# Issuing both stores and then all four loads of a two-batch round, with A and B fetched four batches ahead

## The chip, the core and the metric

The kernel runs on one core of one Trainium2 chip. The metric is device time in microseconds (us) of one execution. The core has a matmul engine (TensorE, PE in the profile), VectorE (DVE), ScalarE (ACT), GpSimd (POOL), and SyncE (SP), which here issues every transfer. All transfers of the loop go through one queue that 16 DMA engines serve. TensorE's granted clock is 1.00 of full speed, that is 2.4 GHz, in every stretch of the loop.

## What is computed

`x` is 64 batches of 128 channels by 2048 time steps, float32. Each batch gets one of 16 conditioning matrices added as a residual, and then one of 64 low-rank adapters (rank 16), again as a residual:

```python
W = weights[condition]                       # (64, 128, 128)
x = x + jnp.einsum('bct,bcd->bdt', x, W)
B_req = B[adapter_ids]                       # (64, 16, 2048)
A_req = A[adapter_ids]                       # (64, 2048, 16)
Bx = jnp.einsum('bni,bri->bnr', x, B_req)    # rank-16 image of each row
x = x + jnp.einsum('bnr,bor->bno', Bx, A_req)
```

For each batch 1024 KB of x come in, 256 KB of A and B (laid side by side by the host) come in, and 1024 KB go out.

## The kernel before

The work is cut into rounds of two batches (ROUND = 2), two rounds to a loop turn (BODY = 4), so 32 rounds in all. They are called r0 to r31 here; round r works on batches b = 2r and b + 1. Four buffers each exist of the input (`x_in`), the output (`x_out`), the A-and-B tile (`ab_in`) and the turned A (`at`); batch b uses number b modulo 4.

TensorE in round r does: `mix_units` for both batches (L376: x times the identity plus W, which gives the first residual F, in four units of 512 columns), `sum_z` for both (L392: F times B, which gives the rank-16 rows z), then `add_low_rank` for the two batches of the round before (L410: A times z). ScalarE copies F out of its banks (L264) and half of z. VectorE in round r, in its program order: `take_z` (L311) for both batches, `add_units` (L318: low-rank part plus F into `x_out`, four units for each batch) for the two batches of the round before, `turn_a` (L327: the transpose of A into `at`) for the two batches of round r. GpSimd picks the matrices and sums the pieces of z.

SyncE follows one order written out by hand in `turn` (L171 to L186) and each of its steps may block all that stand behind it:

- `store(k, b)` waits for the four `add_units` of batch b, then writes batch b out (L159).
- `next_x(k, b)` waits until batch b - 4 has been mixed (`f_made`), then loads x of batch b into the same buffer (L128).
- `next_ab(k, b)` reads the adapter's number, waits for `sum_z` (`z_done`) and `turn_a` (`a_turned`) of batch b - 4, then loads A and B of batch b (L131).

In round r, with b = 2r, the order is: store b - 4, load x of b + 4, store b - 3, load A and B of b + 2 and of b + 3, load x of b + 5. So x is asked for two rounds ahead of its use, A and B one round ahead.

The waits at the other end: `mix_units` waits for `x_loaded`, `sum_z` and `turn_a` for `ab_loaded`, `add_low_rank` for `a_turned`, and `add_units` for `stored`, the landing of the store from the same `x_out` buffer four batches before. The last two batches (from L438 on TensorE, L347 on VectorE) are interleaved by hand.

Of the kernel before, what the change touches and what calls it, by code (L numbers as in the profile page):

```python
# [10 lines left out]
BATCHES, CHANNELS, TIME = 64, 128, 2048  # L11
# [15 lines left out]
ROUND = 2  # L27
BODY = 2 * ROUND
# [11 lines left out]
TURNS = BATCHES // BODY  # L40

def live(count):

    return not (isinstance(count, int) and count <= 0)

def begun(b):

    return not (isinstance(b, int) and b < 0)  # L50
# [7 lines left out]
def cond_lora_residual(nc, x, both_ids, weights, lora, out):  # L58
    with ExitStack() as ctx:
# [57 lines left out]
        def rows_of_z(z_bank, c):  # L117
            return bank[z_bank][TILE * c:TILE * c + RANK, 0:P]
# [3 lines left out]
        @block.sync  # L122
        def _(sp):
            def adapter_of(b):
                return sp.value_load(ids[0:1, 1, bass.ds(b, 1)], min_val=0, max_val=lora.shape[0] - 1)  # L125

            def load_x(k, b):
                sp.dma_start(x_in[k][:], x[b]).then_inc(x_loaded[k], 16)  # L128

            def load_ab(k, adapter):  # L130
                sp.dma_start(ab_in[k][:], lora[adapter]).then_inc(ab_loaded[k], 16)  # L131

            def load_first(i):
                cols = slice(UNIT * i, UNIT * (i + 1) if i < 2 else TIME)
                sp.dma_start(x_in[0][:, cols], x[0, :, cols]).then_inc(first_loaded[i], 16)

            def load_w_first(k):
                cond = sp.value_load(ids[0:1, 0, k:k + 1], min_val=0, max_val=CONDITIONS - 1)  # L138
                sp.dma_start(w_first[k][:], weights[:, cond, :]).then_inc(w_first_in[k], 16)

            sp.dma_start(ids[:].rearrange("p n b -> p (n b)"), both_ids).then_inc(ids_in, 16)
            load_first(0)
            sp.wait_ge(ids_in, 16)
            load_w_first(0)
            load_first(1)
            load_first(2)
            load_w_first(1)
            load_x(1, 1)
            for k in range(ROUND):
                load_ab(k, adapter_of(k))  # L150
            sp.dma_start(w_all[:], weights).then_inc(w_in, 16)
            for k in range(ROUND, BODY):
                load_x(k, k)
            for k in range(ROUND, BODY):
                load_ab(k, adapter_of(k))

            def store(k, b):
                sp.wait_ge(added, UNITS * (b + 1))
                sp.dma_start(out[b], x_out[k][:]).then_inc(stored[k], 16)  # L159

            def next_x(k, b):
                sp.wait_ge(f_made, UNITS * (b - BODY + 1))
                load_x(k, b)

            def next_ab(k, b):
                adapter = adapter_of(b)
                sp.wait_ge(z_done, b - BODY + 1)
                sp.wait_ge(a_turned, b - BODY + 1)
                load_ab(k, adapter)

            def turn(q, last):  # L171
                for kind in range(KINDS):
                    k, other = ROUND * kind, ROUND * (1 - kind)
                    b = BODY * q + k
                    if begun(b - BODY):
                        store(k, b - BODY)
                    if not last:
                        next_x(k, b + BODY)
                    if begun(b - BODY):
                        store(k + 1, b + 1 - BODY)  # L180
                    if begun(b - ROUND) and not (last and kind > 0):
                        next_ab(other, b + ROUND)
                        next_ab(other + 1, b + ROUND + 1)
                    if not last:
                        next_x(k + 1, b + 1 + BODY)

            turn(0, False)
            with sp.Fori(1, TURNS - 1) as q:
                turn(q, False)
            turn(TURNS - 1, True)  # L190

            def store_last(u):
                cols = slice(UNIT * u, UNIT * (u + 1))
                sp.dma_start(out[BATCHES - 1, :, cols], x_out[BODY - 1][:, cols]).then_inc(stored[BODY - 1], 16)

            for k in range(BODY - 1):
                store(k, BATCHES - BODY + k)
            for u in range(1, UNITS):
                sp.wait_ge(evacuated, u)
                store_last(u)  # L200
            sp.wait_ge(added, UNITS * (BATCHES - 1) + 1)
            store_last(0)
            for k in range(BODY):
                sp.wait_ge(stored[k], 16 * (TURNS if k < BODY - 1 else TURNS - 1 + UNITS))
# [99 lines left out]
        @block.vector  # L304
        def _(dve):
            def take_z(i, b, z_bank):
                dve.wait_ge(z_done, b + 1)
                if live(b - 1):
                    dve.wait_ge(z_paired, 2 * (b - 1))
                for c in (1, 3):  # L310
                    nc.vector.tensor_copy(z_part[i][c][:], rows_of_z(z_bank, c)).then_inc(z_taken_dve, 1)  # L311

            def add_units(k, b, turns, banks, units=range(UNITS)):
                if live(turns):
                    dve.wait_ge(stored[k], 16 * turns)
                dve.wait_ge(low_done, b + 1)
                for u in units:
                    nc.vector.tensor_tensor(x_out[k][:, UNIT * u:UNIT * (u + 1)], bank[banks[u]][:], ft[k][u][:],  # L318
                                            ALU.add).then_inc(added, 1)

            def turn_a(k, b, turns):
                dve.wait_ge(ab_loaded[k], 16 * turns)
                if live(b - BODY + 1):
                    dve.wait_ge(low_done, b - BODY + 1)
                flat = ab_in[k][:, 0:JS * RANK + RANK]
                blocks = bass.AP(flat.tensor, flat.offset, [flat.ap[0], [RANK, JS], [1, BLOCK]])
                nc.vector.transpose(at[k][:], blocks).then_inc(a_turned, 1)  # L327

            def normal_round(kind, q):
                b = BODY * q + ROUND * kind  # L330
                for i in range(ROUND):
                    take_z(i, b + i, Z_BANKS[i])
                if begun(b - ROUND):
                    for i in range(ROUND):
                        add_units(ROUND * (1 - kind) + i, b - ROUND + i, q - (kind == 0), LOW_BANKS[kind][i])
                for i in range(ROUND):
                    turn_a(ROUND * kind + i, b + i, q + 1)

            def turn(q):
                for kind in range(KINDS):  # L340
                    normal_round(kind, q)

            turn(0)
            with dve.Fori(1, TURNS - 1) as q:
                turn(q)
            normal_round(0, TURNS - 1)
            take_z(0, BATCHES - 2, Z_BANKS[0])  # L347
            add_units(0, BATCHES - 4, TURNS - 1, LAST_LOW)
            turn_a(BODY - 2, BATCHES - 2, TURNS)
            turn_a(BODY - 1, BATCHES - 1, TURNS)  # L350
            add_units(1, BATCHES - 3, TURNS - 1, LAST_LOW, (0, 1))
            take_z(1, BATCHES - 1, Z_BANKS[0])
            add_units(1, BATCHES - 3, TURNS - 1, LAST_LOW, (2, 3))
            add_units(BODY - 2, BATCHES - 2, TURNS - 1, LAST_LOW)
            add_units(BODY - 1, BATCHES - 1, TURNS - 1, LAST_OWN, (0,))
# [129 lines left out]
```

## Time and profile before

| what | us |
|---|---|
| median of 3 runs | 410.05 |
| lowest, highest | 408.6, 418.84 |
| the profiled execution, its own time | 412.59 |
| its span, first to last instruction | 410.8 |

| engine | busy in the span |
|---|---|
| TensorE matmul | 373.9 us, 91% |
| VectorE | 229.9 us, 56% |
| ScalarE | 238.1 us, 58% |
| GpSimd | 113.6 us, 28% |
| DMA, one queue on 16 engines | 95.0% of their time, 152.19 MB |

The profile is a record of one execution, so sums made from it are made against its own time of 412.59 us. Matmul busy time is a weak measure by itself, as matmuls overlap and their ends are modelled; the distances between the starts of rounds are the better measure. DMA shares are the time that packets took, as a share of 16 engines, and can come out slightly over 1. The time "to landing" of a transfer runs from its issue by SyncE to the last of its completions, so it holds the queueing too.

### The profile page before, as it was taken

What the parts mean: (1) busy time and instruction counts of PE and PEld (TensorE: products, weight loads), DVE (VectorE), ACT (ScalarE), POOL (GpSimd) and SP (SyncE); (2) the same over time, 40 slices, a digit from 0 to 9 for tenths busy, and PEclk for the clock granted to TensorE, in tenths of its full rate; (3) what the DMA queues carried; (4) which work ended last, traced back from release to release, by engine and by line L of the source; (5) the groups of instructions that cost most, each with busy time, mean ns of one, the idle gap of its engine ahead of it and who ended that gap; (6) DMA issues with size and microseconds to landing.
All of it is one profiled execution on the core that took longest, in us unless ns stands there. A gap on an engine that the chain in (4) does not pass through costs nothing.

```text
span 410.8 us, 16881 instructions
## 1 busy us (share of the span) xinstructions
PE 373.9 (91%) x6164; PEld 354.5 (86%) x6164; DVE 229.9 (56%) x445; ACT 238.1 (58%) x580; POOL 113.6 (28%) x263
## 2 busy tenths in 40 slices
PE   8889999999999999999989989898997998989871
PEld 8779999999999999999989979798886897878771
DVE  0116776555566677655556765466753566535762
ACT  2366666656666666665656655566554665546541
POOL 1123333332222333332213333123331133312320
PEclk9899999999999999999999999999999999999995
DMA  6998999999999999999999999999999899999546
GB/s 186 410 372 293 395 409 415 413 412 409 400 408 416 420 410 407 399 421 422 368 422 381 391 416 340 420 335 412 381 350 381 302 410 356 343 392 372 227 167 253
DMA packets 28815, 152.37 MB, mean 371 GB/s; under 512 B 3201, under 2 KB 3458, under 8 KB 12546
## 3 DMA queue, kind: packets, MB, share of 16 engines
q1 hardware_dynamic: 28802, 152.19, 95.0%
q8 instruction: 9, 0.15, 0.1%
q14 instruction: 4, 0.03, 0.0%
HBM read 85.07 MB, written 67.11 MB: 370 GB/s over the span
## 4 chain that ended last, share of the span: by engine, by line
PE 58%; DMA 30%; SPq 4%; issue 3%; DVE 2%; ACT 1%; POOL 1%; ACTq 0%; POOLq 0%; DVEq 0%
PE bank L376 35%; DMA ab_in<-in_lora 28%; PE bank L410 12%; PE bank L392 11%; DMA x_in<-in_x 2%; DVE x_out L318 1%; SPq L125 1%; SPq L159 1%; SPq L128 1%; POOL z_pair L226 0%; DMA ids<-in_ids 0%; DVE z_part L311 0%; SPq L138 0%; ACT x_out L302 0%; SPq L131 0%
## 5 line engine op out<-in xcount | busy, mean ns | idle before, releaser
L376 PE MATMUL bank<-m_sel,x_in 128*128 128x128 f32 x2048 | 240.8, 278 | 3.9 <-DMA x_in<-in_x 2.2
L376 PEld LDWEIGHTS bank<-m_sel,x_in 128*128 128x128 f32 x2048 | 234.1, 193 | 8.7 <-DMA x_in<-in_x 2.6
L264 ACT COPY ft<-bank 128x512 f32<-128x512 f32 x256 | 145.6, 588 | 60.1 <-PE bank L376 58.7
L318 DVE TENSOR_TENSOR x_out<-bank,ft 128x512 f32<-128x512 f32 x253 | 154.3, 680 | 18.5 <-PE bank L410 18.5
L311 DVE COPY z_part<-bank 16x128 f32<-16x128 f32 x128 | 36.8, 287 | 155.1 <-PE bank L392 152.4
L226 POOL TENSOR_TENSOR z_pair<-z_part 16x128 f32<-16x128 f32 x128 | 55.0, 446 | 232.3 <-DVE z_part L311 212.4
L276 ACT COPY z_all<-z_all 16x128 f32<-16x128 f32 x192 | 56.9, 296 | 49.8 <-POOL z_all L231 46.7
L392 PE MATMUL bank<-ft,ab_in 128*16 128x128 f32 x2048 | 64.0, 273 | 20.0 <-DMA ab_in<-in_lora 19.7
L392 PEld LDWEIGHTS bank<-ft,ab_in 128*16 128x16 f32 x2048 | 52.5, 96 | 27.5 <-issue 22.2
L410 PE MATMUL bank<-z_all,at 16*128 16x128 f32 x2048 | 70.0, 284 | 2.5 <-DVE x_out L318 2.5
L410 PEld LDWEIGHTS bank<-z_all,at 16*128 16x128 f32 x2048 | 63.7, 189 | 9.5 <-issue 9.3
L271 ACT COPY z_part<-bank 16x128 f32<-16x128 f32 x128 | 32.9, 257 | 52.3 <-PE bank L392 50.0
L327 DVE STREAM_TRANSPOSE at<-ab_in 128x512 f32<-128x512 f32 x64 | 41.3, 682 | 0.0
L217 POOL TENSOR_TENSOR m_sel<-w_all,ident 128x128 f32<-128x128 f32 x62 | 28.4, 457 | 37.9 <-PE bank L376 19.4
L231 POOL TENSOR_TENSOR z_all<-z_pair 16x128 f32<-16x128 f32 x64 | 28.5, 446 | 7.4 <-POOL z_pair L226 4.5
L418 PE MATMUL bank<-ident 128*128 128x128 f32 x20 | 4.6, 429 | 1.6 <-POOL ident L210 1.6
L418 PEld LDWEIGHTS bank<-ident 128*128 128x128 f32 x20 | 4.3, 331 | 1.6 <-POOL ident L210 1.6
L302 ACT COPY x_out<-bank 128x512 f32<-128x512 f32 x3 | 1.6, 594 | 2.5 <-PE bank L410 2.5
L238 POOL TENSOR_TENSOR m_sel<-w_first,ident 128x128 f32<-128x128 f32 x2 | 0.9, 458 | 6.7 <-DMA w_first<-in_weights 6.7
L264 ACT ACT_TABLE_LOAD x1 | 1.3, 1283 | 0.8 <-PEq L470 0.8
L210 POOL TENSOR_SCALAR_AFFINE_SELECT ident<-ident 128x128 f32<-128x128 f32 x1 | 0.3, 294 | 0.2 <-POOL ident L208 0.2
L208 POOL MEMSET ident<- 128x128 f32 x1 | 0.2, 205 | 0.3 <-POOLq L470 0.3
(5 smaller groups left out, 0.4 us busy)
## 6 DMA issues: line engine op xcount, KB each, us to landing
x_in<-in_x SPq DMA_DIRECT2D x63, 1024.0 KB, 12.7
out<-x_out SPq DMA_DIRECT2D x63, 1024.0 KB, 12.5
ab_in<-in_lora SPq DMA_DIRECT2D x64, 256.0 KB, 12.0
w_all<-in_weights SPq DMA_DIRECT2D x1, 1024.0 KB, 8.0
out<-x_out SPq DMA_DIRECT2D x4, 256.0 KB, 4.8
x_in<-in_x SPq DMA_DIRECT2D x2, 256.0 KB, 3.3
x_in<-in_x SPq DMA_DIRECT2D x1, 512.0 KB, 4.5
w_first<-in_weights SPq DMA_DIRECT2D x2, 64.0 KB, 2.7
```

Source lines behind the costliest of these rows:

```text
L217: nc.gpsimd.tensor_tensor(m_sel[k][:], w_all[:, cond, :], ident[:], ALU.add).then_inc(m_picked, 1)
L226: nc.gpsimd.tensor_tensor(z_pair[i][:], parts[2 * i][:], parts[2 * i + 1][:], ALU.add).then_inc(z_paired, 1)
L231: nc.gpsimd.tensor_tensor(z_all[k][rows_of_unit(0), :], z_pair[0][:], z_pair[1][:], ALU.add).then_inc(z_summed, 1)
L264: nc.scalar.copy(ft[k][u][:], bank[f_bank_of(kind, i, u, final)][:]).then_inc(copied, 1)
L271: nc.scalar.copy(z_part[i][c][:], rows_of_z(z_bank, c)).then_inc(z_taken_act, 1)
L276: nc.scalar.copy(z_all[k][rows_of_unit(u), :], z_all[k][rows_of_unit(0), :]).then_inc(z_placed, 1)
L311: nc.vector.tensor_copy(z_part[i][c][:], rows_of_z(z_bank, c)).then_inc(z_taken_dve, 1)
L318: nc.vector.tensor_tensor(x_out[k][:, UNIT * u:UNIT * (u + 1)], bank[banks[u]][:], ft[k][u][:], ALU.add).then_inc(added, 1)
L327: nc.vector.transpose(at[k][:], blocks).then_inc(a_turned, 1)
L376: last = nc.tensor.matmul(to[:, P * c:P * (c + 1)], x_in[k][:, UNIT * u + P * c:UNIT * u + P * (c + 1)], m_sel[k][:], start=(c == 0), stop ...
L392: last = nc.tensor.matmul(rows_of_z(z_bank, c), ab_in[k][:, first:first + RANK], ft[k][u][:, P * c:P * (c + 1)], start=(u == 0), stop=(u = ...
L410: last = nc.tensor.matmul(bank[banks[u]][:, P * c:P * (c + 1)], at[k][rows, js, :].rearrange("r j i -> r (j i)"), z_all[k][rows, :], start ...
```

## The change

SyncE's order becomes, in round r with b = 2r: store b - 4, store b - 3, load x of b + 4, load x of b + 5, load A and B of b + 4, load A and B of b + 5. A and B are asked for in a later place of the round but two batches further ahead. In VectorE's program `turn_a` of a round's batches comes ahead of `take_z` of the same batches, where it came after `add_units`; the same is done in the hand-written end. The number and size of transfers and the work of every engine are the same.

```diff
             def turn(q, last):
                 for kind in range(KINDS):
-                    k, other = ROUND * kind, ROUND * (1 - kind)
-                    b = BODY * q + k
+                    b = BODY * q + ROUND * kind
+                    slots = range(ROUND * kind, ROUND * (kind + 1))
                     if begun(b - BODY):
-                        store(k, b - BODY)
+                        for i, k in enumerate(slots):
+                            store(k, b - BODY + i)
                     if not last:
-                        next_x(k, b + BODY)
-                    if begun(b - BODY):
-                        store(k + 1, b + 1 - BODY)
-                    if begun(b - ROUND) and not (last and kind > 0):
-                        next_ab(other, b + ROUND)
-                        next_ab(other + 1, b + ROUND + 1)
-                    if not last:
-                        next_x(k + 1, b + 1 + BODY)
+                        for i, k in enumerate(slots):
+                            next_x(k, b + BODY + i)
+                        for i, k in enumerate(slots):
+                            next_ab(k, b + BODY + i)
@@ VectorE
             def normal_round(kind, q):
                 b = BODY * q + ROUND * kind
                 for i in range(ROUND):
+                    turn_a(ROUND * kind + i, b + i, q + 1)
+                for i in range(ROUND):
                     take_z(i, b + i, Z_BANKS[i])
                 if begun(b - ROUND):
                     for i in range(ROUND):
                         add_units(ROUND * (1 - kind) + i, b - ROUND + i, q - (kind == 0), LOW_BANKS[kind][i])
-                for i in range(ROUND):
-                    turn_a(ROUND * kind + i, b + i, q + 1)
@@
             normal_round(0, TURNS - 1)
+            turn_a(BODY - 2, BATCHES - 2, TURNS)
+            turn_a(BODY - 1, BATCHES - 1, TURNS)
             take_z(0, BATCHES - 2, Z_BANKS[0])
             add_units(0, BATCHES - 4, TURNS - 1, LAST_LOW)
-            turn_a(BODY - 2, BATCHES - 2, TURNS)
-            turn_a(BODY - 1, BATCHES - 1, TURNS)
```

## Rows read from the trace of the kernel before

**Rows 1.** The page: TensorE's busy time, and the chain that ended last

```profile
PE 373.9 (91%) x6164; PEld 354.5 (86%) x6164; DVE 229.9 (56%) x445; ACT 238.1 (58%) x580; POOL 113.6 (28%) x263
...
PE 58%; DMA 30%; SPq 4%; issue 3%; DVE 2%; ACT 1%; POOL 1%; ACTq 0%; POOLq 0%; DVEq 0%
```

**Rows 2.** Windows: stretch, length, busy of PE PEld DVE ACT POOL, clock, DMA share, GB/s

```profile
44.51:192.99 148.48, 148.10 (x2501) 140.27 (x2497) 94.03 (x183) 95.63 (x234) 45.80 (x105) 1.00 1.02 412
192.99:370.42 177.43, 160.01 (x2692) 152.46 (x2689) 101.32 (x197) 102.89 (x254) 49.46 (x114) 1.00 0.99 377
...
382.78:410.70 27.92, 15.38 (x256) 14.03 (x256) 15.74 (x28) 9.87 (x25) 3.33 (x8) 0.79 0.59 231
```

**Rows 3.** Waits, whole span: engine line waited for, us in total, times, longest

```profile
PE bank L392 <- DMA ab_in<-in_lora: 19.7, 18, 2.3
```

**Rows 4.** The chain that ended last, in order: start, us, what

```profile
67.37 7.34 PE bank L376 x64
...
90.16 7.34 PE bank L376 x64
...
193.06 3.78 PE bank L376 x32
...
199.42 13.64 DMA ab_in<-in_lora
...
292.38 3.78 PE bank L376 x32
```

**Rows 5.** Tile `x_in`, its two loads issued in 56:67, in 113:124, in 170:181

```profile
DMA to landing us min/median/max: 7.5/8.5/9.4
...
DMA to landing us min/median/max: 9.5/10.4/11.3
...
DMA to landing us min/median/max: 11.6/12.7/13.8
```

**Rows 6.** The DMA view of the stretch 222:228: what it moved, and the queue's share

```profile
DMA packets 256, 1.75 MB, mean 292 GB/s; under 512 B 30, under 2 KB 30, under 8 KB 46
...
q1 hardware_dynamic: 256, 1.75, 99.8%
```

**Rows 7.** Timeline of SyncE in round r14: start, us, engine, line, transfer, count

```profile
171.72 0.35 SPq L159 DMA_DIRECT2D out<-x_out  x1
173.85 0.34 SPq L128 DMA_DIRECT2D x_in<-in_x  x1
174.57 0.35 SPq L159 DMA_DIRECT2D out<-x_out  x1
176.16 1.56 SPq L131 DMA_DIRECT2D ab_in<-in_lora  x2
178.02 0.51 SPq L128 DMA_DIRECT2D x_in<-in_x  x1
```

**Rows 8.** Timeline of VectorE in round r14

```profile
169.05 4.87 DVE L318 TENSOR_TENSOR x_out<-bank,ft 128x512 f32<-128x512 f32 x8 [0.48 <-PE bank L410]
173.84 1.29 DVE L327 STREAM_TRANSPOSE at<-ab_in 128x512 f32<-128x512 f32 x2
178.52 0.61 DVE L311 COPY z_part<-bank 16x128 f32<-16x128 f32 x2 [3.39 <-PE bank L392]
```

**Rows 9.** Timeline of TensorE in round r14

```profile
169.82 7.41 PE L376 MATMUL bank<-m_sel,x_in 128*128 128x128 f32 x64
177.30 1.95 PE L392 MATMUL bank<-ft,ab_in 128*16 128x128 f32 x64
179.18 2.15 PE L410 MATMUL bank<-z_all,at 16*128 16x128 f32 x64
```

**Rows 10.** Timeline of the last round r31: TensorE, then VectorE

```profile
382.78 3.81 PE L376 MATMUL bank<-m_sel,x_in 128*128 128x128 f32 x32
387.86 1.07 PE L392 MATMUL bank<-ft,ab_in 128*16 128x128 f32 x32 [1.28 <-DMA ab_in<-in_lora]
...
395.15 1.29 DVE L318 TENSOR_TENSOR x_out<-bank,ft 128x512 f32<-128x512 f32 x2 [1.29 <-PE bank L410]
```

## The prediction

> **What bounds the kernel now.** I read the page first. TensorE is busy 91% of the span, but the chain that ended last is only 58% TensorE and 30% DMA [rows 1], so the kernel can't have one bound all the way. The windows split it in two. From r3 (44.51) to r16 (192.99), 13 rounds, TensorE is busy for 148.10 of 148.48 us; from there to r30 it is busy 160.01 of 177.43 us, and the DMA share is close to 1 in both [rows 2]. The waits name what TensorE lacks: A and B, for 19.7 us [rows 3]. The chain gives the paces. In the first part the starts 67.37 and 90.16 are two rounds apart, 22.79 us or **11.40 us a round**, TensorE's own pace. From 193.06 (r16) to 292.38 (r24) eight rounds take 99.32 us, **12.42 a round**, with 13.64 us of an A-and-B load as a link of the chain [rows 4].
>
> Why does it start only at r15 or so? The time to landing of the x loads grows while the pace is even: median 8.5 us in r4, 10.4 in r9, 12.7 in r14 [rows 5]. That is 4.2 us in 10 rounds: **the queue falls behind by 0.42 us a round**, so its own pace is 11.82 us a round. The program stays on TensorE's pace only while the lead of its loads lasts. The lead of A and B is the shortest. In r14 their issue starts at 176.16 [rows 7]; `sum_z` of r15 wants them at 177.30 + 11.40 = 188.7 [rows 9]. That is 12.5 us, just what a load then takes.
>
> So there are two nearly equal bounds, TensorE at 11.40 and the queue at 11.82, and once A and B are late a third, the starved pace of 12.42 and more. Over r16 to r31 it is (382.78 - 192.99) / 15 = 12.65 [rows 2, 10]. The starved part also moves fewer bytes, 377 GB/s against 412 [rows 2], and has dips: 292 GB/s over 6 us from 222, with a share of 99.8% [rows 6], which is 6 x (412 - 292) / 412 = 1.8 us lost.
>
> **The lead of A and B (SyncE).** I place the new order in r14, counting from the start of its mix at 169.82 [rows 9]. `add_units` of the two batches before run from -0.77 to +4.10 [rows 8], so the first store goes at +1.9 as before [rows 7] and the second at about +4.2 instead of +4.75. The first x load, now behind both, goes at about +4.9 instead of +4.03 [rows 7]: 0.9 us of its lead of two rounds is lost, while it lands where its place in the queue puts it. The second x load needs the end of the mix, +7.4, and goes then instead of at +8.2. A and B need `sum_z` of their buffer's last user, whose two halves end at about +8.5 and +9.5 [rows 9], and go there instead of at +6.3. Two issues took 1.56 us [rows 7], so SyncE is done by about +10.5 and the next round's first store, at +13.3, doesn't wait for it. The lead: A and B issued at +8.5 are first wanted by `turn_a` two rounds later, at +22.8 + 4.0 = +26.8, so 18.3 us instead of 12.5.
>
> **The transposes (VectorE).** In time they stay where they are, after `add_units`: eight adds, then two transposes of 1.29 us together, then the wait for `sum_z`, 3.39 us of idle [rows 8]. What changes is whose A is turned, now that of the round being mixed. Cost nothing, as they still end about 3.4 us ahead of `take_z`; if that cover went, 1.29 us a round would be late on `take_z` and so on z. The wait for `ab_loaded` now stands ahead of `take_z`; queued behind it are `take_z` and the adds, and behind these the stores. It has 3.4 us of room beyond the landing's deadline. `add_low_rank` gets A 11.4 us earlier than its old margin of 179.18 - 175.13 = 4.0 us [rows 8, 9]; nothing is gained there, as it didn't wait.
>
> **What the queue does then.** Its work is the same, so 11.82 us a round stays: 4608 KB, of which an x load or store is 2.63 us and a pair of A and B 1.3 us. In r14 the last x load is issued at 178.02 and lands 13.8 us on (the longer of the two, as more stands ahead of it), at 191.8 [rows 5, 7]. In the new kernel one more pair of A and B is in the queue in advance, so all of r14's work is done at 191.8 + 1.3 = 193.1; A and B end the round, so the second x lands at 191.8 and the first at 189.2. Wanted: the first x at the start of r16, 169.82 + 22.8 = 192.6 (3.4 us spare), the second half a mix later at 196.3 (4.5 spare), A and B by `turn_a` at 196.6 (3.5 spare). So the first x load is next in line, with **3.4 us spare in r14** where A and B had none. At 0.42 us a round that is 8 rounds: loads of r22 and later are late, felt from r24 on. Stores have more: issued at +4.2, wanted again by `add_units` at about +24.
>
> **What is lost after that.** Low: the queue's steady lag goes on. From r14 to r29, which issues the last loads, it is 15 x 0.42 = 6.3 us, less 3.4 spare: 2.9 us. High: the 7 rounds from r24 to r31 run at the starved pace that before shows in its first eight such rounds, 12.42: 7 x 1.02 = 7.1 us. The dips that make up the difference come when TensorE has stalled and SyncE has issued late; in the new order the first x load is queued behind two stores rather than one, which should leave fewer short queues. No row shows that, so I take the middle, **5.0 us**.
>
> **The sum.** r31 would start at TensorE's pace at 192.99 + 15 x 11.40 = 364.0, less 0.2 us for the first small stalls: 363.8. Plus 5.0 is 368.8. From r31's start to the end the profile has 410.8 - 382.78 = 28.0 us, of which 1.28 is a wait for A and B [rows 10] that now were loaded in r29: 26.7. The transposes in this end gain nothing, as VectorE idled 1.29 us behind them for TensorE [rows 10]. In the start-up A and B of batches 4 and 5 go out earlier, at about 19 us; no wait of TensorE ends on them there, so nothing. The span is 368.8 + 26.7 = 395.5, against 410.8. The profiled execution took 1.8 us more than its span (412.59) and lies 2.5 us above the median: 395.5 + 1.8 - 2.5 = **394.8 us**. With 2.9 or 7.1 in place of 5.0 it is 392.7 or 396.9; its own range is 391.5 to 398.
>
> **Rivals.**
>
> *No stall at all.* If the queue's lag came from the old order (a store behind each x load), it would stop growing. Then 363.8 + 26.7 + 1.8 - 2.5 = **389.8 us**, TensorE's floor. For it: the transfers are within 0.42 us of TensorE's pace, and early in the run the median is only 8.5 us. Against: bytes and engines are the same, and the lag grew as much from r4 to r9 (1.9 us) as after.
>
> *The transfers are slow in the second half whatever the order.* The 377 GB/s would be the queue's own rate there and the starved pace no effect of starving. Then the lag grows by 12.65 - 11.40 = 1.25 us a round from r16 on: 13 rounds to r29 are 16.3 us, less the 2.6 us spare left by r16, 13.7 lost. Span 363.8 + 13.7 + 26.7 = 404.2, **403.5 us**, within 2%. For it: the share is 0.99 even in the slow part, and in the dip to 292 GB/s it was 99.8%, so no lack of work. Against: the slow part begins with the first stalls.
>
> The Trainium skill (DMA: Bandwidth & Descriptors, Bandwidth) holds that for transfers between HBM and SBUF the HBM side binds at about 358 GB/s a core; by that alone the 152.37 MB are an estimated 426 us and no order of issue could help. The trace's 412 GB/s over 148 us disagrees, and HBM Reference (Specifications) of the Trainium skill explains how: a core that streams alone gets about 425 GB/s.
>
> *Grouping hurts.* Two stores and two x loads back to back could make a dip like that at 222 in every round, since it stood where a store was followed by an x load. At 1.8 us each the lag would grow 2.22 us a round: 26 rounds from r3 to r29 are 57.7 us, less the spare of 3.4 + 11 x 0.42 = 8.0: 49.7 lost, **439.5 us**. It makes the kernel slower by 2% (418.3 us) from a lag of 1.4 us a round, that is from about 1.0 us of dip in each. Against: the old order has such a transition in every round too, and ran at 412 GB/s with it.
>
> **Chances.** The forecast with its own range 0.50; no stall 0.17; grouping hurts 0.08; slow second half 0.16; something between the forecast and that, 398 to 402, 0.09. A measurement of this kernel can tell about 2% from no change, 8.2 us: faster is under 401.8. Faster 0.50 + 0.17 + 0.07 = 0.74; same 0.16 + 0.02 = 0.18; slower 0.08. The range runs from the floor, 389, to the slow second half, 403.5, and leaves out the last rival and the edge of that one.
>
> **What would show it.** Right: no wait of `sum_z` for A and B; rounds of 11.40 us until about r24; landing times that grow past 14 us without a stall; then waits of `mix_units` for x, a few us in all; the end from r31 under 27 us. A landing time of x that stops growing shows the first rival, rounds of over 12.4 us from r19 on the second, dips in every round from r3 on the third. Wrong would be a new wait of VectorE for A or for `stored`, or a SyncE that still issues loads when the next adds are done.

## The result, and the profile after

| | before | changed |
|---|---|---|
| median, us | 413.85 (4 runs, 408.6 to 418.84) | 394.69 (4 runs, 394.06 to 398.35) |
| profiled execution, us | 412.59 | 394.86 |
| its span, us | 410.8 | 393.0 |

The ratio is 0.9661 with a 95% interval of 0.9557 to 0.9765: faster by 3.4%, a change clear of the noise. Two of the four runs of before, 417.64 and 418.84 us, were slow ones; they lift its median from 410.05 to 413.85, while the ratio leaves them out and sets 408.6 and 410.05 against the four runs of the changed kernel.

The lines of the kernel file move by one or two from kernel to kernel. In the changed one `mix_units` is L374, `sum_z` L390, `add_low_rank` L408 and `add_units` L316.

The page of the changed kernel, busy times and then the chain that ended last, answers to [rows 1]:

```profile
PE 374.7 (95%) x6164; PEld 352.8 (90%) x6164; DVE 230.2 (59%) x445; ACT 238.5 (61%) x580; POOL 113.2 (29%) x263
...
PE 92%; DMA 2%; issue 1%; DVE 1%; SPq 1%; ACT 1%; POOL 1%; ACTq 0%; POOLq 0%; DVEq 0%
```

TensorE is now 92% of the chain, where it was 58%, and transfers are 2% in place of 30%. The windows (length, busy of PE, PEld, DVE, ACT, POOL, granted clock, DMA share, GB/s) are those of r3 to r16, r16 to r30 and r31 to the end, as in [rows 2]:

```profile
44.99:194.30 149.31, 148.74 (x2501) 140.11 (x2497) 94.05 (x183) 95.89 (x235) 45.80 (x105) 1.00 1.01 410
194.30:354.66 160.36, 160.05 (x2689) 150.91 (x2689) 101.40 (x197) 103.16 (x253) 49.33 (x113) 1.00 1.01 411
...
365.99:393.00 27.01, 15.27 (x256) 13.73 (x256) 14.54 (x26) 9.85 (x25) 3.32 (x8) 0.81 0.62 241
```

Nearly all of the gain is in one place: r16 to r30 take 160.36 us in place of 177.43, TensorE is busy in all of it, and the queue moves 411 GB/s in place of 377. The first part is 0.8 us longer. The two loads of `x_in` issued in r4, in r9, in r14 and in r29, as in [rows 5]:

```profile
DMA to landing us min/median/max: 7.9/7.9/7.9
...
DMA to landing us min/median/max: 9.2/9.3/9.4
...
DMA to landing us min/median/max: 11.2/11.4/11.5
...
DMA to landing us min/median/max: 17.2/17.3/17.4
```

The landings still fall behind, by (11.4 - 7.9) / 10 = 0.35 us a round and then (17.3 - 11.4) / 15 = 0.39, over rounds of 11.46 us ((365.99 - 44.99) / 28). So whatever sets the landings has a pace of 11.81 to 11.85 us a round, the same as before; the section on whose lag it is shows that this is one sixteenth of the queue and not the whole. The backlog is no longer felt, because each load has the lead to outlast it.

### The profile page after: what moved, and what is told of

Read it like the earlier page. It is cut to its first block, busy times and chain, and to the rows that moved or that the text cites. A ratio compares the mean times of both kernels' runs of the same rounds, so it can differ in the third digit from the quotient of the medians.

```text
span 393.0 us, 16867 instructions
## 1 busy us (share of the span) xinstructions
PE 374.7 (95%) x6164; PEld 352.8 (90%) x6164; DVE 230.2 (59%) x445; ACT 238.5 (61%) x580; POOL 113.2 (29%) x263
## 4 chain that ended last, share of the span: by engine, by line
PE 92%; DMA 2%; issue 1%; DVE 1%; SPq 1%; ACT 1%; POOL 1%; ACTq 0%; POOLq 0%; DVEq 0%
PE bank L374 59%; PE bank L408 17%; PE bank L390 16%; DMA x_in<-in_x 2%; DVE x_out L316 1%; POOL z_pair L224 0%; DMA ids<-in_ids 0%; DVE z_part L309 0%; SPq L138 0%; ACT x_out L300 0%; ACT z_all L274 0%; SPq L135 0%; SPq L139 0%; POOL z_all L229 0%; ACT ft L262 0%
## 5 line engine op out<-in xcount | busy, mean ns | idle before, releaser
L374 PE MATMUL bank<-m_sel,x_in 128*128 128x128 f32 x2048 | 240.5, 278 | 5.0 <-DMA x_in<-in_x 2.4
L374 PEld LDWEIGHTS bank<-m_sel,x_in 128*128 128x128 f32 x2048 | 233.7, 193 | 10.5 <-DVE x_out L316 3.2
L316 DVE TENSOR_TENSOR x_out<-bank,ft 128x512 f32<-128x512 f32 x253 | 154.4, 683 | 21.2 <-PE bank L408 21.2
L408 PE MATMUL bank<-z_all,at 16*128 16x128 f32 x2048 | 69.8, 283 | 2.6 <-DVE x_out L316 2.5
L408 PEld LDWEIGHTS bank<-z_all,at 16*128 16x128 f32 x2048 | 63.3, 188 | 9.7 <-issue 9.5
L390 PE MATMUL bank<-ft,ab_in 128*16 128x128 f32 x2048 | 65.7, 274 | 0.8 <-issue 0.8
L390 PEld LDWEIGHTS bank<-ft,ab_in 128*16 128x16 f32 x2048 | 51.4, 96 | 9.8 <-issue 4.2
L325 DVE STREAM_TRANSPOSE at<-ab_in 128x512 f32<-128x512 f32 x64 | 41.5, 687 | 15.2 <-DMA ab_in<-in_lora 15.2
## 6 DMA issues: line engine op xcount, KB each, us to landing
x_in<-in_x SPq DMA_DIRECT2D x63, 1024.0 KB, 11.8
```

The lines of the kernel that those rows point to most:

```text
L374: last = nc.tensor.matmul(to[:, P * c:P * (c + 1)], x_in[k][:, UNIT * u + P * c:UNIT * u + P * (c + 1)], m_sel[k][:], start=(c == 0), stop ...
L390: last = nc.tensor.matmul(rows_of_z(z_bank, c), ab_in[k][:, first:first + RANK], ft[k][u][:, P * c:P * (c + 1)], start=(u == 0), stop=(u = ...
L408: last = nc.tensor.matmul(bank[banks[u]][:, P * c:P * (c + 1)], at[k][rows, js, :].rearrange("r j i -> r (j i)"), z_all[k][rows, :], start ...
```

## Experiments

### The same kernel again, and the lead of A and B without the grouping

`after_again` is the changed kernel unaltered, on the chip of the next three.

> The changed kernel beside the three above, on the same chip. Expected 0.955 to 0.975 of the kernel before, all rounds from r3 to r31 at 11.40 to 11.50 us, x loads that land 7.9 us after issue in r4 and over 16 us in r29.

The median was 396.89 us (393.81 to 398.63), ratio 0.9704 (0.9517 to 0.9891). The execution that was profiled had a span of 396.3 us. Its chain near the end (start, us, what):

```profile
297.16 7.34 PE bank L374 x64
...
308.55 4.75 PE bank L374 x40
313.47 18.51 DMA x_in<-in_x
332.21 7.41 PE bank L374 x64
...
348.57 19.81 DMA x_in<-in_x
368.42 3.84 PE bank L374 x32
```

Here x loads took 18.51 and 19.81 us to land, more than their lead of 18.0 us (the first x load goes 4.9 us into a round and is wanted two rounds after its start, at 22.9). Rounds from r26 on took 11.8 to 12.2 us and r31 began at 368.42, against 365.99 in the first profile. So the changed kernel ends its run at the very edge of the lead of its x loads: one execution just keeps it, another loses some 2.5 us. The expectation of 11.40 to 11.50 us for all rounds was met up to the start of r26 only; that of the ratio, 0.955 to 0.975, was met.

`e1_ab_four_ahead_alternating` undoes the grouping alone:

```diff
-                    if begun(b - BODY):
-                        for i, k in enumerate(slots):
-                            store(k, b - BODY + i)
+                    for i, k in enumerate(slots):
+                        if begun(b - BODY):
+                            store(k, b - BODY + i)
+                        if not last:
+                            next_x(k, b + BODY + i)
                     if not last:
-                        for i, k in enumerate(slots):
-                            next_x(k, b + BODY + i)
                         for i, k in enumerate(slots):
                             next_ab(k, b + BODY + i)
```

> The changed kernel with store and x load alternating again: store, x load, store, x load, then A and B four batches ahead, and the transposes early. Only the grouping is undone. Theory (the lead of A and B is what the change is worth): about the changed kernel's ratio, 0.96 to 0.97 of the kernel before, all rounds at TensorE's pace of 11.40 to 11.46 us, no wait of sum_z for A and B, landing times of the x loads that grow by about 0.4 us a round as in both kernels. Rival (grouping the stores keeps the queue's dips away): dips of some 1.8 us come back, the lag grows by 0.8 us a round or more, the x loads run out of their lead before r20, and the ratio is 0.98 or above.

It took 394.86 us (393.14 to 395.74), ratio 0.9661 (0.9525 to 0.9797), the same as the changed kernel within the spread. From r3 to r31 TensorE was busy in 320.26 of 321.21 us. The theory held: with A and B four batches ahead, the alternating order costs nothing that can be told, although each round has a store followed at once by an x load. The queue is not wholly even here either: in the DMA views of 50:200 and 200:350 the lowest slices of 3.75 us are 336 and 332 GB/s. They are single ones, and TensorE waits for none of them.

### The grouping alone

`e2_stores_grouped_only` is the kernel before with one store moved:

```diff
                     if begun(b - BODY):
                         store(k, b - BODY)
+                        store(k + 1, b + 1 - BODY)
                     if not last:
                         next_x(k, b + BODY)
-                    if begun(b - BODY):
-                        store(k + 1, b + 1 - BODY)
```

> The kernel before with both stores ahead of the first x load and nothing else changed: A and B two batches ahead, in the same place of the queue, transposes late. Theory of the lead: A and B are issued when they were and stand behind the same bytes, so the ratio is 0.99 to 1.01, sum_z waits some 20 us for A and B, from about r15 on. Rival (grouping is what helps): the lag grows more slowly, the waits for A and B are under 8 us and the ratio is under 0.98.

It took 399.03 us (398.01 to 399.9), ratio 0.977 (0.9632 to 0.9907). My theory of the lead fell here: A and B were asked for as late as before, and still most of the gain came, 2.3% where the changed kernel gave 3.0% on the same chip. The intervals of the two overlap widely, so the share is rough. Its waits for A and B:

```profile
PE bank L391 <- DMA ab_in<-in_lora: 7.4, 17, 1.3
```

The number of waits is that of before (17, against 18), but they are short, 7.4 us in place of 19.7 [rows 3]. TensorE's timeline shows two starved rounds of it:

```profile
228.57 7.49 PE L375 MATMUL bank<-m_sel,x_in 128*128 128x128 f32 x64
236.36 1.94 PE L391 MATMUL bank<-ft,ab_in 128*16 128x128 f32 x64 [0.30 <-DMA ab_in<-in_lora]
238.23 2.15 PE L409 MATMUL bank<-z_all,at 16*128 16x128 f32 x64
240.31 7.41 PE L375 MATMUL bank<-m_sel,x_in 128*128 128x128 f32 x64
248.19 1.94 PE L391 MATMUL bank<-ft,ab_in 128*16 128x128 f32 x64 [0.47 <-DMA ab_in<-in_lora]
250.06 2.15 PE L409 MATMUL bank<-z_all,at 16*128 16x128 f32 x64
252.13 1.05 PE L375 MATMUL bank<-m_sel,x_in 128*128 128x128 f32 x7
```

From 228.57 to 252.13 are 23.56 us, 11.78 a round. That is the pace by which the landings fell behind, and it is held to the end. In the kernel before the same state gave 12.42, then more. The GB/s rows of the DMA view of 200:350 (40 slices of 3.75 us) show why, first before, then this kernel:

```profile
GB/s 301 416 423 417 418 425 288 347 428 429 415 404 373 258 412 429 419 416 373 308 341 418 421 391 418 348 262 359 428 393 339 418 303 264 356 429 404 350 420 314
```

```profile
GB/s 381 409 417 365 413 415 382 393 424 382 401 423 404 370 428 417 376 423 424 359 416 418 364 413 428 378 392 421 378 401 424 369 401 427 395 366 431 426 364 423
```

Before, slices of 258 to 314 GB/s come back about every 25 us, two rounds. With the stores grouped none is under 359. So in this pair of kernels, which differ in nothing else, the dips go with the order of store and x load. An alternating order is not enough to bring them on, as e1 shows. Nor does the grouping always keep them away. The kernel `e4_light_pe_new_order` below groups its stores too, and once its x loads are late the same row of 200:350 has slices of 306, 332 and 312 GB/s:

```profile
GB/s 416 425 424 416 429 430 419 425 423 419 429 421 428 425 417 424 417 414 421 421 413 413 390 411 406 391 413 411 406 306 374 424 332 412 427 417 386 425 398 312
```

What brings a dip on stays open.

### The early transposes alone

`e3_transposes_early_only` has the changed kernel's VectorE and the SyncE order of before:

```diff
                 for i in range(ROUND):
+                    turn_a(ROUND * kind + i, b + i, q + 1)
+                for i in range(ROUND):
                     take_z(i, b + i, Z_BANKS[i])
-                for i in range(ROUND):
-                    turn_a(ROUND * kind + i, b + i, q + 1)
```

> The changed kernel's order on VectorE with SyncE's order of before: A is turned in its own round while it is still loaded only two batches ahead. turn_a then wants A 3.4 us earlier than sum_z did. Theory: early transposes bring nothing by themselves; while the loads land by +7 us of their round it costs nothing, and once they land later (from about r14) the two transposes of 1.29 us come behind the landing and ahead of take_z and of the adds, so the last 15 rounds cost up to 1.3 us more each: ratio 1.00 to 1.05. Rival (the early transposes release the A and B buffers sooner and so help): ratio under 0.99.

It took 408.75 us, ratio 1.0006 (0.9944 to 1.0067): nothing. VectorE now stands waiting for A, and longer than for z:

```profile
DVE at L328 <- DMA ab_in<-in_lora: 99.3, 29, 13.0
...
DVE z_part L312 <- PE bank L393: 40.6, 51, 4.8
```

The 99.3 us come out of the time in which it used to wait for `sum_z`. The transposes are no gain themselves. By the program they are a condition of the four-batch lead, as a buffer is free only once its A is turned; no run has SyncE's new order with the late transposes, so what they are worth to it is argued and not measured.

### The queue as the only bound

Four kernels leave out half of the matmuls of `sum_z`, so that TensorE needs less time and the queue sets the pace. They fill a square of the two edits: stores grouped or alternating with the x loads, A and B two or four batches ahead.

```diff
-                for u in range(UNITS):
+                for u in (0, UNITS - 1):
                     for c in range(IN_UNIT):
```

> The changed kernel with half of the matmuls of sum_z left out (units 0 and 3 of 4 only), so that TensorE's own pace falls by about 1.0 us to 10.45 us a round; transfers and the work of all other engines stay. It shows the queue's own pace. Theory (the queue has a pace of 11.83 us a round by itself, and dips to a starved pace of 12.4 come from A and B issued late): from about r8 on the x loads are late and rounds take 11.8 to 12.0 us, and the whole takes 395 to 403 us. Rival (any kernel that waits for the queue falls to the starved pace of 12.4 to 12.7): 410 us or more. Second rival (the lag follows TensorE's pace and the queue is good for 415 GB/s or more): 11.3 us a round, 385 us.

> The kernel before with the same half of sum_z left out. Theory: A and B are late from the first rounds on and the rounds take the starved pace of 12.4 to 12.7 us nearly throughout: 415 to 430 us, slower than the whole kernel before or equal to it although TensorE has less to do. Rival (the queue's pace is one and the same in both orders): the same time as the new order with the light TensorE, within 1%.

> Store, x load, store, x load, then A and B four batches ahead, with half of sum_z left out (units 0 and 3 of 4 only), so that the queue is the bound. With the two light kernels measured so far (old order 402.8 us, new order 390.2) and the next one it fills a square: alternating or grouped, A and B two or four batches ahead. Theory (the dips come where the loop is waiting for the queue and a store is followed at once by an x load): as the x loads run out of lead here too, dips come back in the last third: 393 to 400 us, over the new order. Rival (only the lead of A and B counts): 388 to 392 us, as the new order.

> Both stores first and A and B two batches ahead, with half of sum_z left out (units 0 and 3 of 4 only). Theory (grouping the stores takes the dips away even where A and B are late): rounds settle at the queue's own pace of 11.6 to 11.8 us without rounds over 12.4, the whole 388 to 395 us, well under the 402.8 of the old order. Rival (late A and B bring the dips): 400 to 405 us.

| with the light `sum_z` | A and B two ahead | four ahead |
|---|---|---|
| store and x load alternating | 402.79 (e5) | 393.75 (e10) |
| stores grouped | 395.31 (e11) | 390.19 (e4) |

TensorE's pace fell to 11.01 us a round and not to the 10.45 I had expected, as `sum_z` then waited for ScalarE. The e4 kernel took 390.19 us, under the 395 to 403 expected: its rounds stayed at 11.01 us to r18, had 11.6 us once the x loads were late, and 12.2 to 12.7 in some of the last. e11 fell into step with the landings at r11 and stayed there, at 11.70 us a round. e5 took 402.79 us, under the 415 to 430 of its expectation, but each edit alone again takes 7 to 9 us off, and the two together 12.6.

e4 and e5 ran on one chip, e10 and e11 on another, so the ratios to the kernel before are the safer measure: e5 0.9837 (0.9784 to 0.9891), e10 0.9621 (0.9521 to 0.9721), e11 0.9663 (0.9564 to 0.9762), e4 0.9501 (0.9447 to 0.9555). Against e5 either edit is a clear gain, so the rival that grouping does nothing while A and B are two batches ahead fell. With A and B four ahead the gain of grouping (e4 against e10) is not clear of the noise, as the intervals meet.

Both of these kernels have dips in the last third; in e10 the lowest slices are 272 and 299 GB/s, and its rounds, 11.7 to 11.8 us for four rounds after it began to wait for x, take 12.1 to 12.9 in the last five, at a clock of 1.00.

Part of e5's loss is not the queue. Four of its rounds, in the windows' columns:

```profile
178.77:190.68 11.91, 10.88 (x164) 10.00 (x160) 7.24 (x15) 7.29 (x18) 3.50 (x9) 1.00 0.98 366
190.68:205.93 15.25, 12.99 (x164) 11.74 (x160) 7.97 (x16) 8.49 (x23) 4.95 (x12) 0.84 1.01 413
205.93:219.30 13.37, 13.07 (x164) 12.36 (x160) 6.51 (x14) 6.56 (x15) 2.37 (x7) 0.81 0.72 256
219.30:230.35 11.05, 10.61 (x164) 9.90 (x160) 7.23 (x15) 7.42 (x20) 3.57 (x9) 1.00 1.02 419
```

and TensorE's timeline in them:

```profile
200.51 1.78 PE L392 MATMUL bank<-ft,ab_in 128*16 128x128 f32 x32 [2.25 <-DMA ab_in<-in_lora]
202.23 3.80 PE L410 MATMUL bank<-z_all,at 16*128 16x128 f32 x64
205.96 9.87 PE L376 MATMUL bank<-m_sel,x_in 128*128 128x128 f32 x64
```

Around and after a wait of 2.25 us for A and B the granted clock is 0.84 and 0.81 over two rounds, that is 1.2 GHz for a part of each, and 64 matmuls of `add_low_rank` take 3.80 us in place of 2.14. The queue has caught up meanwhile. The same comes once more in this run: after a wait of 2.48 us at 322.1 the clock of the round from 326.85 is 0.85. In the kernel before and the changed one the clock stays at 1.00 through the loop. In e4 it was 0.87 in two late rounds, from 301.20 and 337.76, after waits of 1.24 and 1.57 us; in e10 and e11 it is 1.00. So the 402.79 can't be put down to the dips in full, and e4's time holds a little of the same loss.

### Whose lag it is

At the end of the changed kernel no load is left, and two stores issued at 356.3 and 358.7 are out. The DMA view of 366.5:368, before the next store is issued at 367.7:

```profile
q1 hardware_dynamic: 11, 0.04, 6.4%
```

A share of 6.4% is one of 16 engines (6.25%). Fifteen had finished and one was still at it. The trace has sixteen completions for each transfer of the loop, and they say the same: of the second of these stores fifteen had come by 366.6, and the last came at 374.65, 8.0 us behind. The same can be read for every load. For the first x load of a round of the changed kernel, in us from its issue:

| issued in | 12 of 16 parts | 15 of 16 | all 16 |
|---|---|---|---|
| r4 | 7.2 | 7.5 | 7.9 |
| r9 | 7.2 | 8.7 | 9.4 |
| r14 | 6.9 | 9.5 | 11.5 |
| r19 | 6.9 | 9.5 | 13.5 |
| r24 | 7.0 | 9.1 | 14.6 |
| r29 | 7.2 | 9.3 | 17.4 |

Three kernels tried to relieve it, on the guess that it is the last one, by cutting each load of A and B in 120 and 8 rows (e7 the kernel before, e8 the changed one, e9 the light e4):

```diff
-                sp.dma_start(ab_in[k][:], lora[adapter]).then_inc(ab_loaded[k], 16)
+                for rows in (slice(0, 120), slice(120, P)):
+                    sp.dma_start(ab_in[k][rows, :], lora[adapter][rows, :]).then_inc(ab_loaded[k], 16)
```

> The kernel before with each load of A and B cut in two transfers, rows 0 to 119 and rows 120 to 127, so that a transfer of 120 rows can be spread over 15 engines of 8 rows and the last engine has none of it; the same bytes, two issues more of SyncE a round for each batch. In the changed kernel's end the queue's share fell to 6.4%, one of 16 engines, with two stores still out, so one engine is behind all others. Theory (the lag of 0.4 us a round is that of one engine, and that engine is the last): its work falls by up to 1.3 us a round, it no longer falls behind, the x loads land within 9 us all the way, sum_z waits under 3 us for A and B, and the kernel runs at 11.40 us a round to the end: ratio 0.955 to 0.97, without any part of the change. Rival (the lag is the whole queue's, or another engine's): the lag grows as before or faster, ratio 0.995 to 1.02.

> The changed kernel with A and B loaded in 120 and 8 rows. Theory of the one engine: the landing times of the x loads stay under 10 us where they grew to over 16, the late waits of mix_units for x that some executions of the changed kernel have go, and the ratio is 0.95 to 0.96, up to 1% better than the changed kernel. Rival: the landing times grow as in the changed kernel and the ratio is 0.965 to 0.975.

> The changed kernel with half of sum_z left out (units 0 and 3 of 4 only) and A and B loaded in 120 and 8 rows. The light kernel without the cut came down to 11.6 us a round once the x loads were late. Theory of the one engine: the other 15 engines carry 11.25 us of packets a round, so the queue's pace becomes 11.2 to 11.4 us and the whole takes 380 to 387 us. Rival: 11.6 us a round and 390 us as without the cut.

All three were far slower: ratios 1.072 (1.0603 to 1.0836), 1.0436 (1.0305 to 1.0566) and 1.05 (1.0399 to 1.0602), 439.55, 432.74 and 432.39 us. The windows of e8:

```profile
60.00:150.00 90.00, 87.52 (x1427) 82.48 (x1420) 54.54 (x106) 54.42 (x136) 27.72 (x64) 0.96 0.99 373
150.00:400.00 250.00, 233.84 (x3689) 221.02 (x3688) 142.52 (x271) 144.29 (x348) 66.73 (x152) 0.95 0.99 369
```

The same bytes at nearly the same share move at 373 GB/s in place of 410, so the cut made the engines' own work dearer: 4.72 MB a round at 373 GB/s are 12.7 us. That is not all of their time, as TensorE's granted clock is lower too, 0.96 and 0.95 in these windows. The cut costs far more than the uneven spread that it was meant to mend. Nor did it end the lag of one part: of the x load of e8 issued at 349.5 fifteen parts landed within 11.4 us and the last after 20.8. Which engine is the slow one stays open.

### The transposes behind the adds

`e6_transposes_next_round` puts `turn_a` of the next round behind `add_units` in VectorE's program:

```diff
                 for i in range(ROUND):
-                    turn_a(ROUND * kind + i, b + i, q + 1)
-                for i in range(ROUND):
                     take_z(i, b + i, Z_BANKS[i])
                 if begun(b - ROUND):
                     for i in range(ROUND):
                         add_units(ROUND * (1 - kind) + i, b - ROUND + i, q - (kind == 0), LOW_BANKS[kind][i])
+                for i in range(ROUND):
+                    turn_a(ROUND * (1 - kind) + i, b + ROUND + i, q + 1 + kind)
```

> The changed kernel with the transposes moved in the program of VectorE behind the adds, for the next round's batches: the order in time is the same, but the loop's branch no longer stands between the adds and the transposes. Theory (the 0.1 us in each turn that TensorE lost against the kernel before comes from where VectorE's branch stands): starts of every second round 22.79 us apart in place of 22.90, 1.4 us less in all, ratio to the changed kernel 0.996. Rival: 22.90 us and no difference.

It took 397.0 us (393.22 to 400.46), ratio 0.9655 (0.96 to 0.9711), no better than the changed kernel. Rounds were 11.48 us in its timeline (204.35 and 215.83 are starts one round apart). The theory about the branch fell. Why the changed kernel's rounds are 0.05 us longer than before's stays open.

## Why the prediction came out right

The time was forecast as 394.8 us and measured as 394.69. That is closer than the steps deserve, and in part luck: two of them were off by about 2.5 us each, in opposite directions.

- **Two close bounds, TensorE at 11.40 and the queue at 11.82.** Right in the numbers. The changed kernel gives 11.46 and 11.81 to 11.85 from its landing times, and e2, which waits for A and B from r15 on, runs at 11.78. What has this pace is not the queue, as I had it, but the slowest sixteenth of it; since a load counts as landed only when its last part has, the sum came out the same.
- **The lead of A and B as what runs out first.** Right, the waits of `sum_z` for A and B are gone from the changed kernel. e1 shows that this lead, with the early transposes, is worth the whole gain without the grouping. That the grouping alone would give most of it as well (e2) was not foreseen; the two don't add up.
- **The spare of the first x load, 3.4 us in r14.** Mis-sized. The first x load of r14 was issued at 176.33 and landed within 11.5 us, at 187.8; wanted at 194.30, it had 6.5 us. Of the 3.1 us between, some 2.4 were there in r4 already: first x landed 12.8 us after that round's start, while the same reckoning from the kernel before (last x at +17.8, less 2.63) gives 15.2. I had charged one more pair of A and B to the backlog, 1.3 us; but in the new order that pair is fetched in the start-up, where the queue has gaps: SyncE issues A and B of batches 4 and 5 at 19.81 instead of 26.59, and the stretch 20:45 moved 358 GB/s in place of 336.
- **5.0 us lost from r24 on.** Not in the first profile, where the last x loads landed in 17.4 us against a lead of 18.0 and r31 began at 365.99; in the second, r31 began at 368.42, against 368.8 forecast. The place was right (the x loads, in the last rounds), the size too large by half or more. My low value of 2.9 was the nearer one.
- **TensorE's floor.** 363.8 forecast for r31; with the rounds 0.05 us longer and the start-up 0.5 us later it was 366.0. This 2.2 us took back part of the point above.
- **The end from r31.** 26.7 forecast, 27.0 measured [rows 10].
- **From span to median.** The span came out as 393.0 and not 395.5. I had taken 2.5 us off as the distance of before's profiled execution (412.59) from its median. That execution did lie above the runs that the ratio counts (408.6 and 410.05), but this was a matter of that one execution and nothing to carry over: the changed kernel's profiled execution, 394.86, lies at its median. The 2.5 us should not have been taken off. This is the error that hid the other.
- **The starved pace of 12.42 as a price of late data.** Half right. It was seen that the dips might belong to the old order, with no row for it. e2 shows that with A and B two batches ahead they do: late data alone costs 11.78 a round there, and the other 0.6 us and more go with the order of store and x load. e4 has dips with the new order, and rounds of 12.2 and 12.6 us (from 288.98 and 325.12) at a clock of 1.00 or 0.99, so the high value of 7.1 us could not be ruled out by the order alone.
- **The rivals.** "Slow in the second half whatever the order" fell with 411 GB/s in r16 to r30. "Grouping hurts" fell with e2, where it helps. "No stall at all" came true for r16 to r31 of the first profile, but not by its mechanism: the lag went on growing as forecast.

## What to carry to other kernels

Where the time to landing of equal loads grows from round to round while the pace is even, something in the transfers is the slower bound already: the difference of two medians over the rounds between gives its pace, and the lead of each load over that growth says when the stall comes. Then look at the single completions of a transfer, as one slow engine of sixteen and a slow queue look the same in the landing time. Give every stream of loads the same lead, since the shortest one sets the moment. And before a starved stretch is priced at what it shows, ask whether its pace is the one by which the landings fall behind: here one moved store brought it from 12.4 us and more to 11.8.

## What the runs showed of the hardware

- One sixteenth of each transfer lands ever later than the rest: in the changed kernel the x load of r4 had fifteen parts after 7.5 us and all after 7.9, that of r29 after 9.3 and 17.4. At the end the share is 6.4%, one of 16 engines, from 366.5 on while two stores are out.
- In the kernel before, with TensorE waiting and stores and x loads alternating, the queue fell to 258 to 314 GB/s for some 4 us about every second round, at a share close to 1 (99.8% over 222:228); with the stores grouped (e2) no slice was under 359. In e4, grouped too, slices of 306 to 332 came late in the run.
- With the 256 KB loads cut in 240 and 16 KB, 64 of each, the queue moved 373 GB/s (e8, 60:150) in place of 410, at nearly the same share (0.99 against 1.01).
- TensorE's granted clock fell to 0.84 and 0.81 over two rounds around a wait of 2.25 us in e5, and to 0.85 in the round after one of 2.48; in e4 it was 0.87 in two rounds after waits of 1.24 and 1.57 us, where waits of up to 2.3 us in the kernel before left it at 1.00. What tells the two apart no run here shows.
